# Two broadcast rows through DRAM instead of TensorE transposes, and a new stage order, in a two-layer graph-attention, routed-MLP and state-space kernel

## What is computed

```python
# layer 0: two graph attentions (the second one masked), then a routed MLP
h1  = gat(relu(x @ mlp1_w), None, W_fc, a_fc);     o = elu(h1) + residual
o   = relu(o @ mlp2_w);  h2 = gat(o, adj, W_hand, a_hand)      # x1 = x + relu(elu(h2) + o)
w   = x1n @ wr + br                                # router weight of each of 256 nodes
idx = top_k(w, 128)[:127];  y = ffn(x1n[idx]) * w[idx]         # scattered back
# layer 1: one more masked attention, then a state-space (Mamba-2) block
e   = leaky_relu(f1[:, None] + f2[None, :]); att = softmax(where(adj > 0, e, -inf)); x3 = x2 + elu(att @ Wh)
out = x3 + mamba2(norm(x3))
```

## Time and profile before

| | us |
|---|---|
| three timed runs | 4077.21, 4076.45, 4078.79 |
| the profiled execution | 4076.81 |
| its span, first to last instruction | 4075.0 |
| TensorE busy | 3816.6 (94%) |
| VectorE busy | 2971.8 (73%) |
| ScalarE busy | 2457.7 (60%) |
| GpSimd busy | 1308.7 (32%) |

### The profile page before, as it was taken

One profiled execution on the slowest core, in us unless ns is written; L12 is line 12 of the kernel. 1 busy time (PEld: TensorE's weight loads), 2 busy tenths in 40 slices (PEclk: granted clock), 3 DMA queues, 4 the chain that ended last, 5 costly groups with the idle time before them and its releaser, 6 DMA issues.

```text
span 4075.0 us, 65950 instructions
## 1 busy us (share of the span) xinstructions
PE 3816.6 (94%) x21784; PEld 3371.5 (83%) x21784; DVE 2971.8 (73%) x7987; ACT 2457.7 (60%) x5762; POOL 1308.7 (32%) x2073
## 2 busy tenths in 40 slices
...
GB/s 91 11 28 26 34 36 23 31 36 23 31 36 23 31 36 25 30 36 36 23 31 36 23 31 36 23 31 36 23 31 36 33 24 34 36 23 31 37 16 26
DMA packets 73631, 126.81 MB, mean 31 GB/s; under 512 B 9600, under 2 KB 64256, under 8 KB 65408
## 3 DMA queue, kind: packets, MB, share of 16 engines
...
## 4 chain that ended last, share of the span: by engine, by line
PE 71%; POOL 11%; issue 6%; DVE 6%; ACT 4%; POOLq 1%; DMA 0%; DVEq 0%; ACTq 0%
PE A L1185 11%; PE M L1386 9%; PE Q L1302 6%; PE A L1174 6%; PE A L1223 6%; PE M L1403 6%; PE A L1205 5%; POOL dt_w L564 5%; PE A L1232 3%; PE M L1341 3%; PE Q L1232 3%; PE Q L1270 3%; PE M L1375 2%; PE A L1215 1%; PE Q L1291 1%
## 5 line engine op out<-in xcount | busy, mean ns | idle before, releaser
L595 POOL TENSOR_TENSOR xdt<-xr,dt 128x1024 f32<-128x1024 f32 x64 | 226.3, 3536 | 1182.3 <-ACT xr L793 1182.3
L1185 PE MATMUL A<-w_fc,o1T 128*128 128x256 f32 (+1 forms) x2048 | 460.9, 383 | 45.6 <-ACT o1T L632 45.6
L1185 PEld LDWEIGHTS A<-w_fc,o1T 128*128 128x128 f32 x2048 | 383.4, 190 | 112.8 <-ACT o1T L632 61.3
L804 ACT ACTIVATE dec<-cumB,cumcol 128x256 f32<-128x256 f32 (+1 forms) x1024 | 367.7, 451 | 12.0 <-issue 12.0
L1386 PEld LDWEIGHTS M<-xdt,dec 128*128 128x128 f32 x3072 | 364.4, 197 | 11.7 <-issue 7.3
L1386 PE MATMUL M<-xdt,dec 128*128 128x64 f32 x3072 | 362.1, 280 | 7.3 <-POOL xdt L595 6.2
L675 ACT ACTIVATE o2T<-A,c_mlp 128x256 f32<-128x256 f32 x128 | 53.7, 470 | 453.8 <-PE A L1223 453.8
L1067 DVE SCALAR_TENSOR_TENSOR acc<-M,w_conv,acc 128x255 f32<-128x255 f32 (+2 forms) x768 | 315.6, 473 | 0.2 <-ACT acc L747 0.2
L1321 PE MATMUL M<-xT_m,w_in 128*128 128x256 f32 x1280 | 287.0, 380 | 0.5 <-DVE tz L1103 0.5
L1321 PEld LDWEIGHTS M<-xT_m,w_in 128*128 128x128 f32 x1280 | 243.8, 191 | 33.2 <-DVE tz L1103 0.9
L1302 PE MATMUL Q<-selT,w_up 128*128 128x128 f32 x2048 | 262.3, 283 | 0.3 <-ACT selT L735 0.3
...
## 6 DMA issues: line engine op xcount, KB each, us to landing
cumB<-cum_dram SPq DMA_DIRECT2D x64, 1024.0 KB, 4.7
x_in<-in_x SPq DMA_DIRECT2D x64, 256.0 KB, 2.8
x<-in_x SPq DMA_DIRECT2D x64, 256.0 KB, 5.0
out<-x3b SPq DMA_DIRECT2D x64, 256.0 KB, 2.2
...
w_up<-in_L_ffn_w SPq DMA_DIRECT2D x1, 1024.0 KB, 10.0
w_down<-in_L_ffn_w SPq DMA_DIRECT2D x1, 1024.0 KB, 10.9
```

Of the source, the lines that this page charges most:

```text
L804: last = nc.scalar.activation(dec[:, h, :], columns[:, h, :], ACT.Relu, bias=cumcol[:, i, h:h + 1], scale=-1.0)
L1185: last = nc.tensor.matmul(rows1(half, u, 2), o1T[:, k, u * P:(u + 1) * P], w_fc[:, k, half, 0:D + 2 * i], start=(k == 0), stop=(k == KH - 1))
```

## The change

f2 of part g and the router weights no longer pass through TensorE. The steps `g_bcast` (TensorE) and `q_route` (TensorE and ScalarE) are gone. Two steps of the sync queue, `g_spread` and `q_spread`, store the column of 256 values to DRAM, wait until it has landed, and load it as a row into 128 partitions (128 KB). `q_route_col` becomes one small addition on VectorE, `q_rank` and `g_mask` wait for the loads. Three more waits are added (`before` in `a_norm`, in `q_gather` and in `q_route_col`), `junk` becomes twice as large. And `STEPS` is another table for all engines: TensorE's lags now go from 0 to 5, so that it runs 69 turns.

```diff
--- before.py
+++ after.py
@@ -27,36 +27,36 @@
 
 STEPS = {
     "tensor": [
-        ("a_fc.0", 1), ("a_fc.1", 1), ("q_gather", 2), ("a_bcast", 1), ("g_pturn", 3), ("q_ffn1.0", 2), ("m_cb", 4),
-        ("m_xrow", 4), ("g_att", 3), ("a_att.0", 1), ("a_att.1", 1), ("m_y.0", 4), ("m_y.1", 4), ("a_uturn", 1),
-        ("q_ffn1.1", 2), ("a_mlp2", 1), ("m_yturn", 4), ("b_proj", 1), ("m_turn", 3), ("m_out", 4), ("b_bcast", 1),
-        ("m_z", 3), ("q_ffn2", 2), ("b_pturn", 1), ("b_res", 1), ("q_scatter", 2), ("b_att", 1), ("m_xbc_a", 3),
-        ("m_xbc_b", 3), ("m_da", 3), ("g_turn", 2), ("a_turn", 0), ("m_cum_col", 3), ("g_proj", 2), ("a_mlp1.0", 0),
-        ("g_bcast", 2), ("a_mlp1.1", 0), ("q_route", 1),
+        ("m_xbc_a", 5), ("b_pturn", 2), ("m_xbc_b", 5), ("b_att", 2), ("g_att", 4), ("b_res", 2), ("q_ffn1.0", 3),
+        ("m_da", 5), ("a_mlp1.0", 1), ("a_mlp1.1", 1), ("m_cum_col", 5), ("q_ffn1.1", 3), ("a_fc.0", 1),
+        ("a_fc.1", 1), ("m_cb", 5), ("a_bcast", 1), ("m_xrow", 5), ("q_ffn2", 3), ("a_att.0", 1), ("a_att.1", 1),
+        ("q_scatter", 3), ("m_y.0", 5), ("m_y.1", 5), ("g_turn", 3), ("a_uturn", 1), ("g_proj", 3), ("m_yturn", 5),
+        ("a_mlp2", 1), ("m_out", 5), ("b_proj", 1), ("m_turn", 4), ("q_gather", 2), ("b_bcast", 1), ("m_z", 4),
+        ("a_turn", 0), ("g_pturn", 3),
+    ],
+    "vector": [
+        ("m_stats", 5), ("m_mix.1", 6), ("q_x2", 4), ("q_route_col", 3), ("g_stats", 4), ("a_elu_c", 2),
+        ("g_norm", 4), ("m_y.0", 6), ("m_y.1", 6), ("a_uturn", 2), ("g_proj", 4), ("a_stats", 0), ("q_rank", 3),
+        ("m_norm", 5), ("m_out", 6), ("b_proj", 2), ("g_mask", 4), ("g_lrelu", 4), ("g_max", 4), ("b_mask", 2),
+        ("b_lrelu", 2), ("g_pturn", 4), ("b_max", 2), ("m_gate", 5), ("b_pturn", 2), ("m_conv_b.0", 5),
+        ("m_conv_b.1", 5), ("b_elu_c", 2), ("b_x1", 2), ("m_scan", 5), ("g_elu_b", 4), ("a_norm", 0), ("q_stats", 2),
+        ("m_conv_b.2", 5), ("q_gelu_a", 3), ("m_cum_col", 5), ("q_gelu_b", 3), ("m_silu", 5), ("a_fc", 1),
+        ("q_norm", 2), ("q_ffn2", 3), ("a_fcol", 1), ("m_cb", 5), ("a_maxima", 1), ("q_route", 2), ("g_x3", 4),
+        ("a_probs", 1), ("m_mix.0", 5), ("q_scatter", 3), ("a_att", 1),
     ],
     "scalar": [
-        ("m_xbc_a", 3), ("g_turn", 2), ("a_turn", 0), ("m_xbc_b", 3), ("g_proj", 2), ("a_mlp1", 0), ("q_route", 1),
-        ("m_decay.0", 3), ("m_silu", 3), ("g_exp", 2), ("q_gather", 1), ("a_fcol", 0), ("g_pturn", 2),
-        ("a_factors", 0), ("m_xrow", 3), ("m_decay.1", 3), ("a_att", 0), ("a_elu_b", 0), ("g_elu", 2), ("g_att", 2),
-        ("a_mlp2", 0), ("m_yturn", 3), ("q_gelu_a", 1), ("m_gated", 3), ("m_turn", 2), ("b_proj", 0), ("q_gelu_c", 1),
-        ("m_z", 2), ("m_dt_exp", 2), ("b_exp", 0), ("b_pturn", 0), ("b_att", 0), ("b_elu_b", 0),
-    ],
-    "vector": [
-        ("a_probs", 2), ("m_mix.0", 5), ("a_att", 2), ("m_mix.1", 5), ("a_elu_c", 2), ("g_elu_b", 4), ("a_uturn", 2),
-        ("m_y.0", 5), ("m_y.1", 5), ("g_x3", 4), ("m_stats", 4), ("q_gelu_a", 3), ("m_norm", 4), ("b_proj", 2),
-        ("q_gelu_b", 3), ("m_out", 5), ("b_mask", 2), ("q_ffn2", 3), ("b_lrelu", 2), ("b_max", 2), ("a_stats", 1),
-        ("m_gate", 4), ("q_scatter", 3), ("b_pturn", 2), ("q_x2", 3), ("g_stats", 3), ("g_norm", 3), ("b_elu_c", 2),
-        ("b_x1", 2), ("a_norm", 1), ("m_scan", 4), ("q_stats", 2), ("m_conv_b.0", 4), ("g_proj", 3), ("q_norm", 2),
-        ("m_cum_col", 4), ("q_route", 2), ("g_mask", 3), ("m_conv_b.1", 4), ("q_route_col", 2), ("m_conv_b.2", 4),
-        ("g_lrelu", 3), ("q_rank", 2), ("g_max", 3), ("a_fc", 1), ("a_fcol", 1), ("m_silu", 4), ("a_maxima", 1),
-        ("g_pturn", 3), ("m_cb", 4),
+        ("a_elu_b", 1), ("g_turn", 3), ("m_yturn", 5), ("m_gated", 5), ("a_mlp2", 1), ("g_proj", 3), ("b_proj", 1),
+        ("m_turn", 4), ("g_exp", 3), ("m_z", 4), ("b_exp", 1), ("m_dt_exp", 4), ("g_pturn", 3), ("m_xbc_a", 4),
+        ("b_pturn", 1), ("m_xbc_b", 4), ("q_gather", 2), ("b_att", 1), ("b_elu_b", 1), ("a_turn", 0), ("g_att", 3),
+        ("g_elu", 3), ("a_mlp1", 0), ("m_silu", 4), ("q_gelu_a", 2), ("q_gelu_c", 2), ("m_decay.0", 4), ("a_fcol", 0),
+        ("a_factors", 0), ("m_xrow", 4), ("m_decay.1", 4), ("a_att", 0),
     ],
     "gpsimd": [
-        ("a_norm", 6), ("m_da", 9), ("q_norm", 7), ("m_xrow", 9), ("q_turn", 7), ("m_turn", 9), ("m_norm", 8),
-        ("m_rms", 9), ("m_dt", 8), ("m_dt_log", 8), ("g_norm", 7),
+        ("m_dt_log", 6), ("m_da", 6), ("q_norm", 3), ("m_turn", 6), ("m_xrow", 6), ("g_norm", 4), ("a_norm", 0),
+        ("m_norm", 5), ("m_rms", 6), ("m_dt", 5), ("q_turn", 3),
     ],
     "sync": [
-        ("a_load", 0), ("m_spread", 3), ("a_residual", 0), ("m_store", 3),
+        ("m_spread", 6), ("a_load", 0), ("q_spread", 3), ("a_residual", 2), ("g_spread", 4), ("m_store", 6),
     ],
 }
...
@@ -180,6 +180,7 @@
         sc = {k: sb(f"sc_{k}", [P, U, N]) for k in "bg"}
         nmax = {k: sb(f"nmax_{k}", [P, U]) for k in "bg"}
         lr = pr = sc
+        fc_row = sb("fc_row", [P, N])
         rs = {k: sb(f"rs_{k}", [P, U]) for k in "bg"}
         rr = {k: sb(f"rr_{k}", [P, U]) for k in "bg"}
         pT = {k: sb(f"pT_{k}", [P, U, N]) for k in "bg"}
...
@@ -237,6 +238,8 @@
         x3b = sb("x3b", [P, U, D])
         x4 = x3b
         cum_dram = nc.dram_tensor("cum_dram", [NH, N], F32, kind="Internal").ap()
+        fc_dram = nc.dram_tensor("fc_dram", [1, N], F32, kind="Internal").ap()
+        w_dram = nc.dram_tensor("w_dram", [1, N], F32, kind="Internal").ap()
 
 
         A0, A1, A2 = bank("A0"), bank("A1"), bank("A2")
...
@@ -509,12 +514,29 @@
                 sp.wait_ge(cum_stored, 16 * b)
                 sp.dma_start(cumB[:], cum_dram.partition_broadcast(P)).then_inc(cum_spread, 16)
 
+            def g_spread(b):
+                sp.wait_ge(S["g_fc"], b)
+                sp.dma_start(fc_dram.rearrange("h (u p) -> p (h u)", p=P), fc["g"][:, :, 1],
+                             allow_slow_non_contiguous=True).then_inc(fc_stored, 16)
+                sp.wait_ge(fc_stored, 16 * b)
+                sp.dma_start(fc_row[:], fc_dram.partition_broadcast(P).rearrange("q h n -> q (h n)")).then_inc(fc_spread, 16)
+
+            def q_spread(b):
+
+                sp.wait_ge(S["wcol_ready"], b)
+                sp.dma_start(w_dram.rearrange("h (u p) -> p (h u)", p=P), wcol[:], allow_slow_non_contiguous=True)\
+                    .then_inc(w_stored, 16)
+                sp.wait_ge(w_stored, 16 * b)
+                sp.dma_start(wrow[:], w_dram.partition_broadcast(P).rearrange("q h n -> q (h n)")).then_inc(w_spread, 16)
+
             def m_store(b):
                 sp.wait_ge(S["x4_ready"], b)
                 sp.dma_start(out[b - 1].rearrange("(u p) d -> p u d", p=P), x4[:]).then_inc(out_stored, 16)
 
-            turns(sp, "sync", dict(a_load=a_load, a_residual=a_residual, m_spread=m_spread, m_store=m_store))
-            sp.wait_ge(cum_stored, 16 * B)
+            turns(sp, "sync", dict(a_load=a_load, a_residual=a_residual, m_spread=m_spread, m_store=m_store,
+                                    g_spread=g_spread, q_spread=q_spread))
+            for stored in (cum_stored, fc_stored, w_stored):
+                sp.wait_ge(stored, 16 * B)
             sp.wait_ge(out_stored, 16 * B)
 
         @block.gpsimd
...
@@ -724,11 +746,6 @@
                                                 scale=rr["g"][:, u:u + 1])
                 last.then_inc(S["g_eb"], 1)
 
-            def q_route(b):
-                act.wait_ge(S["w_ps"], b)
-                nc.scalar.activation(wrow[:], Q0[:, 0:N], ACT.Identity, bias=c_route[:, 0:1])\
-                    .then_inc(S["wrow_ready"], 1)
-
             def q_gather(b):
                 act.wait_ge(S["sel_ps"], b)
                 nc.scalar.copy(pickT[:], Q0[:, 0:N])
...
@@ -848,6 +865,8 @@
             def norm(k, src):
                 def step(b):
                     v.wait_ge(S[f"{k}_rstd"], nth(b, 2, 2))
+                    if k == "a":
+                        before(v, S["a_xT_ps"], b)
                     for u in range(U):
                         last = nc.vector.tensor_scalar(xn[k][:, u, :], src[:, u, :], mv[k][:, u, 0:1],
                                                        rstd[k][:, u:u + 1], ALU.subtract, ALU.mult)
...
@@ -919,12 +938,12 @@
                     last.then_inc(S[f"{k}_fc"], 1)
                 return step
 
-            def mask(k, ps, m):
-                def step(b):
-                    v.wait_ge(S[f"{k}_fb_ps"], b)
+            def mask(k, row, m):
+                def step(b):
+                    v.wait_ge(*((fc_spread, 16 * b) if k == "g" else (S[f"{k}_fb_ps"], b)))
                     for u in range(U):
                         last = nc.vector.scalar_tensor_tensor(out=sc[k][:, u, :], in0=m[:, u, :],
-                                                              scalar=fc[k][:, u, 0:1], in1=ps[:, N:2 * N],
+                                                              scalar=fc[k][:, u, 0:1], in1=row,
```

(29 more changed lines are left out.)

13 lines of the change are left out of this document (6 added, 7 removed).

## The result

The changed kernel takes 4541.9 us (median of 4 runs, 4538.05 to 4544.04), against 4077.71 us (4 runs of the kernel before, measured beside it). That is 1.1136 times the time, with an interval of 1.1122 to 1.115: 464 us slower, where 93 us faster was forecast. The profiled execution has a span of 4542.3 us. A full turn takes 67.2 us on average, where 60.29 stood before. In what follows, one execution of the kernel with pieces of 8 bytes is left out: it took 5337 us at a mean granted clock of 0.695, against 0.98 in that kernel's other executions.

A forecast was written before the change was run, and what follows sets the result against it. TensorE, 94% busy, was taken as the bound. 63.5 to the first start, 224 filling, 59 turns of 58.3 (3440), then 43, 160 and 52 sum to 3982.5; forecast 3984 us, range 3935 to 4072.

The forecast's parts named there:

- the landing of the store: Column of 256 single elements stored to DRAM: 2.3 us, 5.9 in a full queue, taken from loads of 512 elements.
- The load: 128 KB row load from DRAM after each store: 2.8 us, up to 4.7.
- The round trips: Column ready to row landed, through DRAM on the sync queue: 5.5 us, at most 11.0, costed at nothing.
- The cover: VectorE work ahead of `q_rank` and of `g_mask` that hides the round trips: about 9 us each.
- the fourth rival: Slow single-element store: each us of round trip above about 11 delays VectorE; 4161 us at 14; chance 0.03.
- four filling intervals: First four intervals between `a_mlp1` starts while the pipeline fills: 54, 56, 56.5 and 57.5, together 224 us.
- last three `m_z` intervals: Draining the pipeline after `m_z` of graph 61: 56, 54 and 50 us.
- The long way around TensorE: From `m_xbc_b` to `a_att` over ScalarE and VectorE: 25.0 us, 1.0 more than TensorE's 24.0 of work.
- rival 1: TensorE without a gap, the long way 0.8 us faster: turn of 57.5, total 3937 us; chance 0.15.
- rival 2: Long way is longer, other just-in-time gaps cost 0.4 to 1.5 us a turn: 4008 to 4072 us; chance 0.22.
- Rival 3: ScalarE and VectorE set the turn, through a late `m_decay.0` or late taps: 4120 us at 2.3 more; chance 0.07.
- rival 5: Only the transposes go, waits find other places: turn of 59.85, total 4075 us, no change; chance 0.03.

The follow-up runs named there:

- the kernel with one slow store: Changed kernel with 8-byte pieces for the router weights alone, f2 still stored as 256 pieces of 4 bytes: 4261.74 us, 1.0448 of the kernel before.
- kernel with 8-byte pieces: Changed kernel with each column stored as 128 pieces of 8 bytes in place of 256 of 4: 3951.99 us, 0.9687 of the kernel before.
- the two kernels in the new order: Changed kernel's stage order with both rows made on TensorE again, 4030.8 us; and the same order with the 8-byte stores, 3951.99 us.

## Why the prediction was wrong

*The step that failed is the landing of the store.* The prediction took 2.3 us, with 5.9 as its upper end; it was 8.2 for the router weights and 10.6 for f2. The two rows it went by, `n_col` and `c_mlp`, are loads of single elements from DRAM into the chip's memory, four to a partition. They say nothing of single elements that are written side by side to DRAM. No row of the trace showed such a write, and the bound from both sides was drawn with rows of one side only. The stores with 8 bytes or more from piece to piece landed in 1.5 to 3.3, so they stay within the stated 2.3 to 5.9 or below it; the one that the change makes does not. The load was mis-sized too: 5.1 and 4.7 against the 2.8 taken, with 4.7 as its upper end.

*The round trips.* Stated were 5.5 us, at most 11.0; they took 14.8 and 17.9. The cover was judged nearly rightly, 9 us each. VectorE had room for the router row from 2011.94 to about 2020.0, 8 us. For f2 the kernel with one slow store shows it: store and load of 13.5 us (8.6 and 4.9) and a wait of 4.6 (297.3 over 64) leave some 9. But then the upper end of 11.0 was never covered, and the fourth rival's limit of 11 us contradicts the 9. In the kernel with 8-byte pieces, whose rows arrive in some 7.5 us, neither wait is left in the full turns, apart from one of 0.7 us. The router row has only half a us to spare.

*The fourth rival* was the right mechanism with too small a chance (0.03) and the wrong price. It said that every us above 11 costs one us a turn. Measured is 9.2 us a turn more than with quick stores, for 3.8 and 6.9 us above 11. Two things were missing. The two trips are in series: the sync queue starts the second store when the first has landed, and the prediction had "the second's column is not there before", which was true only for a short store. Separating the steps gave back 5.2 us a turn. And TensorE ran at a lower clock behind its idle time. The matmuls are the same in number (21528), but TensorE is busy for 3959.5 us with the slow stores and 3767.6 with the quick ones, 3.0 us a turn. In the turn shown, 2.93 us of it lie in the stretch at a granted clock of 0.56 behind the 4.5 us of idle time, where the twelve matmuls of `m_xbc_a` took 4.7 us in place of 2.6. These matmuls stand on the way from `g_mask` to the next router column, and by the rows above the turn is longer by the whole 2.93.

*The rest of the sum.* With the stores made quick, the total is close to what the prediction described:

| | forecast | 8-byte pieces |
|---|---|---|
| a full turn | 58.3 | 57.95 |
| wait at `a_turn`, at `a_fc` | none | none |
| wait before `g_turn` | in time | 0.20 |
| idle time before `a_att` | 0.5 | none |
| end of `m_xbc_b` to `a_att`, beyond TensorE's work | 1.0 | 0.25 |
| four filling intervals, total | 224 | 221.7 |
| last three `m_z` intervals | 160 | 149.2 |
| last `m_z` to the end | 52 | 53.4 |
| total | 3984 | 3952 |

59 times 0.35 us and 11 us of draining are the difference. That the turn came so close is in part luck. The long way around TensorE to `a_att`, the last term of the turn, was mis-sized: from `b_att` at 2076.57 to `a_att` of the next turn (2042.87 + 57.95) it is 24.25 us, against 24.0 of work, so 0.25 us were lost there and not 1.0. The chain that ended last goes around TensorE here too, but comes back at `g_turn`, 10 us later, where the wait of 0.20 stands. Of the 57.95, then, 57.5 are left without these two losses, 0.2 more than the 57.27 of the prediction. The measured turn lies between the forecast and rival 1 (57.5), the total nearer to rival 1's 3937; rival 2 did not come. Rival 3 stays without a trace, and rival 5 is refuted by the two kernels in the new order.

*The page of the Trainium skill* that I weighed, "DMA: Bandwidth & Descriptors", section "Rules for kernel authors", spoke against this store, and I gave it too little weight. It says that such a store becomes one descriptor for each element, and that the last dimension should be made contiguous. The trace agrees: the kernel with 8-byte pieces moves 16384 fewer packets under 512 bytes (30080 against 46464), which is 128 for each of the 128 stores, and the contiguous row was the quickest of all, with 1.1 us. But the number of elements does not give the price: 256 of them landed in 1.5 us when they lay apart, and in 8.2 side by side.
